# A longer pipeline in a cross attention, and the experts' sum moved into the next layer

## The reference, cut to what matters

```python
x = ln(x + L0_attn(x))                       # "a"
x = ln(x + L0_xattn(x, ctx, ctx, side, mask))# "b": 16 heads of 8, 77 context rows
x = ln(x + L0_ffn(x))                        # "m": shared experts + top 2 of 8
x = ln(x + L1_attn(x))                       # "s": selective state-space scan, 16 states
x = ln(x + L1_xattn(x, ctx, ctx))            # "c"
x = ln(x + L1_ffn(x))                        # "q"
```

## Time and profile before

| | us |
|---|---|
| median of three runs | 3356.13 (3353.65 to 3359.01) |
| the profiled execution, its own time | 3354.66 |
| its span | 3352.8 |
| first cross attention with its barriers | 184 to 653 |
| routing, shared and routed experts | 658 to 1206 |
| experts' sum, statistics, opening of the scan | 1206 to 1303 |
| scan | 1303 to 2260 |
| second cross attention, last layer | 2260 to 3352 |

### The profile page before, as it was taken

How to read it: one execution, slowest core, us unless ns; L and a number is a source line. 1 busy time by engine, 2 the same in 40 slices (tenths; PEclk the granted TensorE clock), 3 DMA queues, 4 the chain that set the end, 5 groups by cost and what they waited for, 6 DMA issues and landing times. The chain is left out here.

```text
span 3352.8 us, 51512 instructions
## 1 busy us (share of the span) xinstructions
PE 2726.7 (81%) x16584; PEld 1624.9 (48%) x16584; DVE 2409.3 (72%) x3855; ACT 1716.0 (51%) x3206; POOL 2033.2 (61%) x1795
## 2 busy tenths in 40 slices
PE   7868888799788817888798788868999999997555
PEld 5545555455455512333333333325777777775222
DVE  6968888655433344999989999885666666665777
ACT  7746666533222205656566665534444444443665
POOL 5447777556545546999989999862333333333444
PEclk9979999889899958899988998889999999998555
DMA  6810000011044433334333333310000000000000
GB/s 208 334 21 18 17 18 16 4 34 38 32 140 137 126 107 139 139 140 151 131 147 139 141 151 128 149 63 16 5 3 5 5 3 5 5 3 1 13 16 22
DMA packets 130121, 249.21 MB, mean 74 GB/s; under 512 B 41057, under 2 KB 97910, under 8 KB 109314
## 3 DMA queue, kind: packets, MB, share of 16 engines
q1 hardware_dynamic: 119250, 228.98, 19.9%
q0 software_dynamic: 9088, 16.94, 1.5%
q10 hardware_dynamic: 1584, 0.79, 0.1%
HBM read 189.34 MB, written 59.13 MB: 74 GB/s over the span
## 5 line engine op out<-in xcount | busy, mean ns | idle before, releaser
L1819 POOL TENSOR_TENSOR s_drive<-s_du,s_b_sb 128x1024 f32<-128x1024 f32 x256 | 599.0, 2354 | 35.3 <-DVE s_state_ps L2066 34.8
L2179 PE MATMUL s_y_ps<-s_read,w_ident 128*128 128x512 f32 x832 | 451.6, 673 | 163.2 <-DVE s_read L2079 163.0
L2066 DVE TENSOR_TENSOR_SCAN s_state_ps<-s_decay_ps,s_drive 128x512 f32<-128x512 f32 x416 | 486.6, 1215 | 98.0 <-ACT s_decay_ps L1965 87.0
L1965 ACT ACTIVATE s_decay_ps<-s_delta,neg_rate 128x508 f32<-128x508 f32 x512 | 346.4, 685 | 316.0 <-DVE s_state_ps L2066 266.0
L2179 PEld LDWEIGHTS s_y_ps<-s_read,w_ident 128*128 128x128 f32 x832 | 158.6, 204 | 426.6 <-DVE s_read L2079 266.2
L2417 ACT ACTIVATE c_pT<-c_turn_ps 77x512 f32<-77x512 f32 x256 | 149.1, 587 | 244.8 <-PE c_turn_ps L2618 244.5
L2079 DVE TENSOR_TENSOR s_read<-s_state_ps,s_c_sb 128x1024 f32<-128x1024 f32 x208 | 254.7, 1224 | 7.2
L2373 POOL TENSOR_TENSOR c_p<-c_p,c_norm 128x1232 f32<-128x1232 f32 x64 | 143.8, 2247 | 156.5 <-DVE c_norm L2498 156.5
L1422 POOL DMA_INDIRECT m_y_scratch<-e_y,e_index x156 | 152.6, 978 | 134.5 <-DVE e_index L1456 59.9
L2351 POOL TENSOR_TENSOR x<-c_xs,w_c_bo 128x128 f32<-128x128 f32 x64 | 30.8, 482 | 304.6 <-DVE c_xs L2458 304.6
L747 ACT ACTIVATE b_pT<-b_turn_ps 77x512 f32<-77x512 f32 x256 | 145.5, 591 | 120.1 <-PE b_turn_ps L872 120.1
(11 more groups left out here) (371 smaller groups left out, 6931.2 us busy)
## 6 DMA issues: line engine op xcount, KB each, us to landing
s_b_sb<-s_bc_scratch SPq DMA_DIRECT2D x64, 1024.0 KB, 4.7
s_c_sb<-s_bc_scratch SPq DMA_DIRECT2D x64, 1024.0 KB, 4.7
m_rows_scratch<-fill SPq DMA_DIRECT2D x33, 1040.0 KB, 27.5
e_w<-in_m_we_dram SPq DMA_DIRECT2D x39, 384.0 KB
e_xg<-m_rows_scratch SPq DMA_DIRECT2D x39, 260.0 KB
k_y<-m_y_scratch SPq DMA_DIRECT2D x32, 256.0 KB, 3.6
out_dram<-q_result SPq DMA_DIRECT2D x16, 256.0 KB, 2.3
x<-in_x_dram SPq DMA_DIRECT2D x13, 256.0 KB, 2.8
```

The lines of the kernel that those rows point to most:

```text
L1819: nc.gpsimd.tensor_tensor(drive[:, (g * states + n) % drives, :, :], du[:, s, :, :], b_sb[:, n, :].unsqueeze(1).broadcast_to([128, halves, ...
L1965: nc.scalar.activation(decay[:, m, :, 1:], delta[:, s, m, :].rearrange("p (b t) -> p b t", t=T)[:, :, 1:], ACT.Exp, scale=core.neg_rate[:, ...
L2066: nc.vector.tensor_tensor_scan(home[:, h, :], decay[:, h, :, :].rearrange("p b t -> p (b t)"), drive[:, (g * states + n) % drives, h, :], ...
L2179: last = nc.tensor.matmul(y_ps[:, m, :], core.ident[:, :], read[:, r % deep, m, :], start=False, stop=False)
```

## The change

1. In the first cross attention five slots instead of four and six for `v_own`; xT, q, k and v are made five elements ahead, the scores four, maximum and exponential three, sums and division two. ACT normalises six ahead, first in its step instead of last. All steps are written out, without the hardware loop.
2. `v_own` becomes 4 x 128 columns that are cleared once, by DVE at the start of the phase; per element DVE copies the 128 columns of v, eight by eight, to columns 128 j + 32 r (part j, quarter r), and the matmul of part j and quarter r reads 32 columns from 32 r + 120 j, in which all but the eight of its head are zero. The mask and its load go.
3. `combine_experts` and the `finish_statistics` behind it go. In the scan's block SP loads the results into the four `read` slots ahead of its other work; DVE adds both to x, takes the statistics and finishes them in three batches (group 0; groups 1 and 2; groups 3 to 15), with three roots in ACT's list. The experts' two sets of landing semaphores are taken for the whole kernel's length. The clearing of `decay` moves to the front of DVE's list.

```diff
-    slots = 4
+    slots, v_slots = 5, 6
-        v_own = sb("b_v_own", [S2, slots, per, 128])
+        v_own = sb("b_v_own", [S2, v_slots, per * 128])
...
         def around(eng, step):
-            for i in range(-5, 5):
-                step(i, i % slots)
-            with eng.Fori(5, B - 10, slots) as i:
-                for k in range(slots):
-                    step(i + k, (1 + k) % slots)
-            for i in range(B - 7, B + 1):
+            for i in range(-6, B + 1):
                 step(i, i % slots)
...
             def step(i, s):          # ACT
-                if on(i, 4):
-                    copy_xT(i + 4, s)
+                if on(i, 6):
+                    normalise(i + 6, (s + 1) % slots)
+                if on(i, 5):
+                    copy_xT(i + 5, s)
...
-                if on(i, 2):
-                    exp(i + 2, (s + 2) % slots)
+                if on(i, 3):
+                    exp(i + 3, (s + 3) % slots)
                 if on(i, 0):
                     copy_c(i, s)
-                if on(i, 5):
-                    normalise(i + 5, (s + 1) % slots)
...
+            nc.vector.memset(v_own[:, :, :], 0.0).then_inc(prepared.sem, 1)
...
             def values(i, s):
-                if behind(i, slots):
-                    dve.wait_ge(mixed.sem, mixed.at(i - slots, per))
-                nc.vector.tensor_tensor(v_own[:, s, :, :], v_ps.unsqueeze(1).broadcast_to([S2, per, 128]),
-                                        core.w["b_v_mask"][0:S2, :, :], ALU.mult).then_inc(v_ready.sem, 1)
+                if i == 0:
+                    dve.wait_ge(prepared.sem, prepared.at(0, 2))
+                if behind(i, v_slots):
+                    dve.wait_ge(mixed.sem, mixed.at(i - v_slots, per))
+                own = v_own[:, i % v_slots, :].rearrange("p (j r c) -> p j r c", j=per, r=quads)[:, :, :, 0:dk]
+                nc.vector.tensor_copy(own, v_ps.rearrange("p (r j c) -> p j r c", r=quads, j=per)
+                                      ).then_inc(v_ready.sem, 1)
...
             def step(i, s):          # DVE; PE's and POOL's likewise
-                if on(i, 2):
-                    bias_max(i + 2, (s + 2) % slots)
+                if on(i, 3):
+                    bias_max(i + 3, (s + 3) % slots)
                 if on(i, -1):
                     leave(i - 1, (s - 1) % slots)
-                if on(i, 1):
-                    sums(i + 1, (s + 1) % slots)
-                if on(i, 4):
-                    keys(i + 4, s)
-                    values(i + 4, s)
+                if on(i, 2):
+                    sums(i + 2, (s + 2) % slots)
+                if on(i, 5):
+                    keys(i + 5, s)
+                    values(i + 5, s)
...
+        batches = (range(0, 1), range(1, 3), range(3, NG))
...
+            def load_y(g):           # SP, scan
+                if g >= deep:
+                    sp.wait_ge(combined.sem, combined.at(g - deep, 2))
+                for k in range(2):
+                    slot = y_in[k][g % deep]
+                    sp.wait_ge(slot.sem, slot.at(g // deep, 0))
+                    first = k * B * T + g * GT
+                    sp.dma_start(read[:, g % deep, k, :].rearrange("p (b d) -> p b d", b=GB),
+                                 core.y_dram[first:first + GT, :].rearrange("(b p) d -> p b d", b=GB)
+                                 ).then_inc(slot.sem, 16)
...
+            for g in range(NG):
+                load_y(g)
             store_rows(0)
...
+            take_root(0)             # ACT, scan
             normalise(0, 0)
+            take_root(1)
             copy_xT(0, 0)
             normalise(1, 1)
...
             open_conv(1, 1)
+            take_root(2)
             around(act, body)
...
+            def combine(g):          # DVE, scan
+                here = x[:, g * GB:(g + 1) * GB, :].rearrange("p b d -> p (b d)")
+                for k in range(2):
+                    slot = y_in[k][g % deep]
+                    dve.wait_ge(slot.sem, slot.at(g // deep, 16))
+                    if k:
+                        dve.wait_ge(combined.sem, combined.at(g, 1))
+                    nc.vector.tensor_tensor(here, here, read[:, g % deep, k, :], ALU.add).then_inc(combined.sem, 1)
+                dve.wait_ge(combined.sem, combined.at(g, 2))
+                for j in range(GB):
+                    done = nc.vector.bn_stats(core.stats[:, g * GB + j, :], x[:, g * GB + j, :])
+                done.then_inc(combined.sem, 1)
...
+            combine(0)
+            fold(0)
+            combine(1)
+            refine(0)
+            combine(2)
+            fold(1)
+            combine(3)
+            refine(1)
+            for g in range(4, NG):
+                combine(g)
+            fold(2)
+            refine(2)
```

More of the change, by code:

```diff
@@ L883, in mix @@
                     cols = slice(32 * r, 32 * r + 32)
-                    last = nc.tensor.matmul(c_ps[cols, :], v_own[:, s, j, cols], pT[:, j, r, :],
+                    first = 32 * r + (128 - dk) * j
+                    last = nc.tensor.matmul(c_ps[cols, :], v_own[:, i % v_slots, first:first + 32], pT[:, j, r, :],
                                             start=(j == 0), stop=(j == per - 1))
@@ L1656, in phase_scan @@
         f0_ps, f1_ps = f_ps[:, 0, :], f_ps[:, 1, :]
+        gap = sb("s_first_gap", [128, B])
+        root = sb("s_first_root", [128, B])
+        batches = (range(0, 1), range(1, 3), range(3, NG))
+        y_in = [[sig(f"s_y_in{k}{n}", 16) for n in range(deep)] for k in range(2)]
+        combined = sig("s_combined", 3)
+        folded = sig("s_first_folded", 9)
+        rooted = sig("s_first_rooted")
         cleared = sig("s_cleared", 2)
@@ L1864, in _, with take_root @@
             nc.scalar.activation(decay_rate[:, :, :], core.w["s_A_log"][:, :, :], ACT.Exp).then_inc(rates.sem, 1)
+            def take_root(n):
+                own = slice(batches[n].start * GB, batches[n].stop * GB)
+                act.wait_ge(folded.sem, folded.at(n, 4))
+                nc.scalar.activation(root[:, own], core.rstd[:, own], ACT.Sqrt).then_inc(rooted.sem, 1)
             def normalise(g, s):
-                if isinstance(g, int) and g == 0:
-                    act.wait_ge(prepared.sem, prepared.at(0, 1))
+                for n, batch in enumerate(batches):
+                    if g in batch:
+                        act.wait_ge(folded.sem, folded.at(n, 9))
                 if behind(g, 1):
@@ L2024, in _ @@
         def _(dve):
[L2026 to L2027 removed]
+            nc.vector.memset(decay[:, :, :, 0:1], 0.0).then_inc(prepared.sem, 1)
             nc.vector.tensor_tensor(
@@ new lines, in refine @@
+            def refine(n):
+                own = slice(batches[n].start * GB, batches[n].stop * GB)
+                rstd = core.rstd[:, own]
+                dve.wait_ge(rooted.sem, rooted.at(n, 1))
+                nc.vector.reciprocal(root[:, own], root[:, own]).then_inc(folded.sem, 1)
+                dve.wait_ge(folded.sem, folded.at(n, 5))
+                nc.vector.tensor_tensor(gap[:, own], rstd, root[:, own], ALU.mult).then_inc(folded.sem, 1)
+                dve.wait_ge(folded.sem, folded.at(n, 6))
+                nc.vector.scalar_tensor_tensor(gap[:, own], gap[:, own], -0.5, root[:, own],
+                                               ALU.mult, ALU.mult).then_inc(folded.sem, 1)
+                dve.wait_ge(folded.sem, folded.at(n, 7))
+                nc.vector.scalar_tensor_tensor(rstd, gap[:, own], 1.5, root[:, own],
+                                               ALU.add, ALU.mult).then_inc(folded.sem, 1)
+                dve.wait_ge(folded.sem, folded.at(n, 8))
+                nc.vector.scalar_tensor_tensor(shift[:, own], core.mean[:, own], -1.0, rstd,
+                                               ALU.mult, ALU.mult).then_inc(folded.sem, 1)
```

125 lines of the change are left out of this document (43 added, 82 removed).

## The result

Run beside the kernel before on one chip, the changed kernel took 3240.59 us (median of four, 3237.50 to 3243.32) and the kernel before 3354.89 us (median of four, 3348.59 to 3359.01): a ratio of 0.9651, 95% interval 0.9637 to 0.9666. That is 114 us less, where 91 were forecast, and 2 us under the low end of the range. The sign and both mechanisms held; the largest term was too small.

A forecast was written before the change was run, and what follows sets the result against it. A loop over PE and ACT was taken to set the cross attention's pace, with DVE 0.6 us under it, and almost nothing to overlap at the seam. Gains 62 + 29 = 91 us: 3356 - 91 = 3265 us, range 3243 to 3302.

The forecast's parts named there:

- Cross attention, the mean step: First cross attention: mean step falls from 6.89 to 5.91 us over 63 steps, a gain of 61.7 us.
- The clean step: First cross attention: a step without dips takes 5.8 us, as three loops lie at 5.70 to 5.8.
- The POOL chain: First cross attention: bias addition through lowering, exponential, projecting and DVE's work, 11.5 us over two steps, 5.8 each.
- The PE and ACT loop: First cross attention: projecting to exponential, normalising, copy of xT and back to PE, summed to 5.70 us.
- The 0.11 a step for clock dips and fill: First cross attention: some 7 us left for PE clock dips and cold first steps, 0.11 per step.
- The rival with a new wait: First cross attention: a new wait replaces the old one, mean step 6.5, total 3302 us; chance 0.17.
- The loop written out at nothing: First cross attention: writing out the hardware loop costs nothing, because unrolled steps run at 6.69 us.
- The drain at 0: End of the first cross attention, after the last bias addition: keeps its length, 0 us, bounds plus and minus 4.
- Seam, 31.8 for 29: Between experts and scan: first normalising 34.6 us sooner, chain pays 5.7, gain 29 us, ends 22 and 33.
- DVE has cover: Scan's opening: DVE's 44 us of work ends near 1258 (1266 with 8 lost), before ACT's third root at 1270.7.
- as a rival had it: Seam becomes DVE's: combines pass at 4 us a group, seam gives 18 instead of 29, 3276 us; chance 0.07.
- The store on SP: Scan's opening: store of B and C rows, queued behind all 32 loads, may slip a few us, covered.

The follow-up runs named there:

- masked_v: The changed kernel with v made again by the 512-wide multiplication with the mask, still six slots; ratio 0.9725 to the kernel before.
- flat: The kernel before with only the hardware loop of the first cross attention written out; 3270.76 us, ratio 0.9976 to the kernel before.
- old_depth: The changed kernel with the old depth and four slots in the cross attention, but normalising first, v copied with six slots, steps written out; ratio 0.9841.
- seam_only: The kernel before with only the new seam (experts' sum in the scan's opening), old cross attention; 3252.05 us, ratio 0.9915 to the kernel before.
- norm_last: The changed kernel with ACT's normalising moved back to the end of its step, new depth kept; ratio 0.9828 to the kernel before.
- flat_v: The changed kernel with the old order and depth of the cross attention, but steps written out and v copied with six slots; ratio 0.9854.
- one_batch: The changed kernel with all sixteen groups in one batch, all additions and statistics before the first normalising; 3185.62 us, ratio 0.9723 to the kernel before.
- late_root: The changed kernel with the third batch's square root and its DVE correction moved into the first group's scans; 3160.41 us, ratio 0.9639.
- x_only: The kernel before with only the new first cross attention, old seam; 3193.82 us, ratio 0.9738 to the kernel before.

## Why the prediction was right or wrong

**Cross attention, the mean step: this term failed.** I forecast 5.91 and it was 5.60; 63 x 0.31 = 19.5 of the 23 us missed (114 for 91). Two parts of the working are at fault.

- *The clean step, 5.8 for 5.61: 12 us.* I summed DVE's step to 5.74, subtracting the idle time the profile gives before the masks (0.62), and adding the copy as a busy time, 0.27. Both mix records with places. In the step of the earlier trace rows the keys, whose row is below, start at 621.77 and have a place of 0.37 (406.13 to 406.50 in the changed kernel), so DVE is free from 622.14, 0.71 before the masks. With 0.71 and a place of 0.20 the same sum is 6.69 - 0.71 - 0.60 + 0.20 = 5.58 us, near the 5.53 that masked_v gives. The POOL chain, 11.5 over two steps, contained two estimates of together 4 us, and I let it set the value. The PE and ACT loop, 5.70 from rows alone, was the nearest, and it is the one that sets the pace. It was 0.09 too long for the same reason as DVE's sum: it took normalising to its recorded end, and the copy of xT starts 0.10 before that (402.51, where the record of 402.12 ends at 402.61).

```profile
621.77 0.45 DVE L783 SCALAR_TENSOR_TENSOR b_k_own<-b_in_ps,w_b_bk,w_head_mask 128x308 f32<-128x308 f32 x1
```

- *The 0.11 a step for clock dips and fill: 7 us.* The old kernel has steps of 8.2 to 8.4 us now and then, and so has flat. In the changed kernel there is none between 220 and 540 us; its granted clock is 1.00 in 300 to 500 us. The irregular first steps (3.70, 6.37, 5.02, 7.09) average 5.55, no more than the rest.

The mechanism was right: the wait for xs went, turning x has none, and the loop that I had summed from rows is what is left. The choice of the longest sum, and the allowance on top of it, were wrong. "DVE is the busiest engine, 33 of 40 us" misread: there PE has 33.27 and DVE 32.98. The rival with a new wait did not come, though old_depth shows it was near: with the old depth the division takes the place of the normalising. The prediction had given the division a whole step of room, and its rival did not name it.

**The loop written out at nothing** was wrong by 6.7 us, for the better: flat shows it. It is part of the 81. The cover I named, that unrolled steps ran at 6.69, was itself the sign of the gain: they were 0.15 under the loop's 6.84.

**The drain at 0, with ends of 4,** was 1.9 for the better. **The clearing of v_own** took 2.6 us, not 3.6, and was hidden: the first bias addition came at 193.75 instead of 194.22.

**Seam, 31.8 for 29.** Loads began 2.7 us later than before against the last scatter (3.6 forecast); the first normalising was 36.0 sooner (34.6). The chain from there to the first decay paid 3.6 (5.7), but not by its forecast terms:

- The second root and the table load cost 1.2 us together up to the first tanh, against 1.9.
- From there to the copies of the projection it gave back 1.8, which I had not counted. The four matmuls of L2184 took 1.98 us; before, they took 3.78, with the granted clock at 0.50, the lower level (1.2 GHz), in that window, against 0.93 in the window shown above. In seam_only, where they also took 1.98, it is 1.00, the upper level (2.4 GHz), in 1171 to 1173. The same instructions, on the path, at another clock. The change does not give this for sure: nine of the ten kernels with the new opening in three batches took 1.98 here, but norm_last took 3.78, and its stretch from last scatter to first scan is 75.6 us where flat_v on the same chip has 73.1. The three with the old seam took 3.77 or 3.78, and one_batch, without the overlap, 1.98. Why the clock differs is open.

```profile
1280.88 3.78 PE L2161 MATMUL s_f_ps<-s_dtT,w_s_dt_proj 17*128 17x512 f32 x4 [1.29 <-ACT s_dtT L1934]
```

```profile
1164.04 1.98 PE L2184 MATMUL s_f_ps<-s_dtT,w_s_dt_proj 17*128 17x512 f32 x4 [1.29 <-ACT s_dtT L1895]
```

- From there to the first decay it paid 4.2, against 2.8 for the root and its tables plus a share of POOL's 1.0: 1.2 of it is the wait for DVE.

Then the first scan waited for the correction, 0.65 more than before: 36.0 - 3.6 - 0.65 = 31.8. **"DVE has cover" was wrong.** I gave three pairs of fold and refine 2.4 us each. The last fold alone ran from 1179.00 to 1186.50, 7.5 us, since I had charged the port to the wide additions only (one pair did take 4.22 instead of 1.47) and not to narrow operations, each of which can lose a whole POOL operation. The wide ones behaved as forecast: four pairs, of 4.22, 2.72, 3.43 and 2.73 us instead of 1.47, lost 7.2 us, and 8 had been allowed. So the seam did turn into DVE's at its very end, as a rival had it, but not by that rival's way: most groups passed at 2.3 us, not 4, and it was the last fold that was late. The price was some 2.5 us, by late_root, instead of 11. The store on SP behaved as forecast: it went out at 1166.94, right behind the loads, and nothing waited.

**The sum.** 91 forecast, 117.1 between the profiled executions: 22 more from the cross attention, 3 from the seam, 1.6 from stages whose code is the same. The range began at 3243 because it took 5.7 us as the best mean step (and 76 us for 63 x 1.19, which is 75). Its bound "it can't be under DVE's 5.6" was the right end and should have been the low end. That would have given 3238.

## What to carry to other kernels

Sum an engine's step from start to start, not from durations: a record's length holds a tail in which the next instruction can already have started, and the idle time shown before a waiting instruction leaves that tail out. Where two waits of nearly the same length stand in different loops, expect little from breaking one (here 2.7 and 16.9 us) and the whole from breaking both (63.8), and look for the second by asking what is next at the moment the first is gone. When work is slid under another engine's, put the narrow operations at its end where the other engine's wide ones can't hold them, since a 0.2 us operation can cost as much as the one it meets.

## What the runs showed of the hardware that was not expected

- Narrow DVE operations of 52 columns took 2.21 to 2.42 us beside POOL's of 2.35, and 0.20 to 0.28 for 64 columns alone.
- The copy of 77 x 128 from PSUM, recorded as 0.28 us, holds DVE for 0.20; the 512-wide multiplication, recorded as 0.68 to 0.69, for 0.59 to 0.60.
- Long steps of 8.2 to 8.4 us, in the old kernel and in flat, are absent in flat_v, where PE is as busy (82.97 against 81.87 of 100 us in 400 to 500) and only the v operation and its slots differ. The granted clock there is 1.00, against 0.98 in flat. Why is open.
- The experts' part took 466 us on two chips and 537 to 543 on the others, with the same instructions. The windows from first to last scatter, of x_only and of the changed kernel, show 218 us at a granted clock of 1.00 and 259 at 0.95, with about the same busy time of POOL; what holds the slower one was not looked into:

```profile
822.00:1040.00 218.00, 210.79 (x1047) 137.71 (x1044) 97.52 (x264) 62.19 (x111) 151.57 (x155) 1.00 0.52 147
```

```profile
856.20:1115.20 259.00, 225.28 (x1045) 145.35 (x1044) 94.53 (x264) 60.84 (x111) 151.60 (x156) 0.95 0.43 123
```
